# Six transformer layers: the order of pieces in the loops of TensorE, VectorE, ScalarE and GpSimd laid out anew

## What is computed

```
qkv = shift(x) @ Wqkv;  q, k = l2norm(q) * qs, l2norm(k) * ks;  q, k = rotary(q), rotary(k)
p   = softmax(8 * q @ [k_prev_window, k_window] + mask);  x = (p @ [v_prev, v]) @ Wo + x
xn  = layernorm(shift(x)) * g + b;  a, gate = split(xn @ W1 + b1);  x = a * gelu(gate) @ W2 + b2 + x
```

## Time and profile before

| | |
|---|---|
| three runs | 3569.05, 3572.99, 3574.07 us; median 3572.99 |
| the profiled execution | 3574.2 us, span 3572.4 us |
| busy share of the span | PE 94%, PEld 75%, DVE 78%, ACT 71%, POOL 79% |
| mean granted TensorE clock | 0.977 |

### The profile page before, as it was taken

The page is one execution under the profiler, slowest core; times in us unless marked ns, Lnnn a source line. Parts: engine busy times, 40 slices in busy tenths (PEclk is TensorE's granted clock), DMA queues, the critical chain, the costliest instruction groups (busy, mean ns, idle before and its releaser), DMA issues.

```text
span 3572.4 us, 148602 instructions
## 1 busy us (share of the span) xinstructions
PE 3355.3 (94%) x64228; PEld 2680.4 (75%) x64228; DVE 2803.0 (78%) x4876; ACT 2546.0 (71%) x4688; POOL 2810.5 (79%) x3469
## 2 busy tenths in 40 slices
PE   4798897999999999999999999999999999999997
PEld 2555554778788888787888888887888887888875
DVE  3386667888888888888888888888888888888873
ACT  3333224778788888888887887887888888887863
POOL 1355646988898888898888888888888888888871
PEclk9898999999999999999999999999999999999998
DMA  3332221211121111122111221112111112111110
GB/s 103 103 104 77 86 57 41 57 41 43 40 56 44 48 40 46 40 53 52 44 40 47 51 53 38 43 44 51 46 47 42 41 45 53 40 44 48 38 43 25
DMA packets 126732, 183.45 MB, mean 51 GB/s; under 512 B 29824, under 2 KB 61440, under 8 KB 126080
## 3 DMA queue, kind: packets, MB, share of 16 engines
q1 hardware_dynamic: 119232, 146.15, 16.3%
q0 software_dynamic: 6848, 27.80, 2.6%
HBM read 59.01 MB, written 14.16 MB: 20 GB/s over the span
## 4 chain that ended last, share of the span: by engine, by line
PE 82%; POOL 6%; issue 4%; DVE 3%; ACT 2%; DMA 1%; another core or an unknown queue 0%; SPq 0%; POOLq 0%; ACTq 0%; DVEq 0%
PE bank L565 21%; PE bank L628 10%; PE bank L639 9%; PE bank L601 7%; PE bank L575 5%; PE bank L585 5%; PE bank L612 4%; PE bank L702 3%; PE bank L680 3%; PE bank L691 3%; PE bank L478 1%; PE bank L538 1%; PE bank L648 1%; PE bank L517 1%; PE bank L543 1%
## 5 line engine op out<-in xcount | busy, mean ns | idle before, releaser
L565 PE MATMUL bank<-wqkv,xs 128*128 128x512 f32 x3456 | 1045.2, 420 | 8.3 <-DVE m L1096 5.1
L1868 POOL TENSOR_TENSOR m<-m 128x512 f32<-128x512 f32 x576 | 753.0, 1316 | 28.1 <-DVE m L1096 27.5
L565 PEld LDWEIGHTS bank<-wqkv,xs 128*128 128x128 f32 x3456 | 590.2, 191 | 99.7 <-DVE m L1096 7.2
L1107 DVE TENSOR_REDUCE ss<-sq 128x8 f32<-128x512 f32 x768 | 505.8, 670 | 98.1 <-ACT sq L1465 97.7
L1096 DVE TENSOR_TENSOR m<-bank,tab 128x512 f32<-128x512 f32 x768 | 521.5, 679 | 2.5 <-POOL m L1868 2.5
L1465 ACT ACTIVATE sq<-bank 128x512 f32<-128x512 f32 x768 | 454.6, 599 | 64.8 <-PE bank L565 45.3
L1876 POOL TENSOR_TENSOR S<-S,nw 128x1024 f32<-128x1024 f32 x192 | 367.5, 1914 | 112.0 <-DVE S L1127 107.7
L628 PEld LDWEIGHTS bank<-P,big 64*64 64x64 f32 x24576 | 378.8, 135 | 94.6 <-issue 93.5
L1884 POOL TENSOR_TENSOR S<-S,rs 128x512 f32<-128x512 f32 x384 | 396.3, 1048 | 32.1 <-DVE rs L1141 31.6
L1094 DVE TENSOR_TENSOR m<-bank,tab 128x512 f32<-128x512 f32 x576 | 391.7, 680 | 36.2 <-PE bank L585 19.5
L628 PE MATMUL bank<-P,big 64*64 64x32 f32 x24576 | 401.9, 220 | 7.0 <-issue 6.5
(11 more groups left out here) (229 smaller groups left out, 6566.5 us busy)
## 6 DMA issues: line engine op xcount, KB each, us to landing
big<-vst SPq DMA_DIRECT2D x1536, 64.0 KB, 2.0
stage<-in_wqkv SPq DMA_DIRECT2D x36, 256.0 KB, 3.0
tab<-in_tab SPq DMA_DIRECT2D x48, 128.0 KB, 2.2
xsort<-big SPq DMA_DIRECT2D x4, 960.0 KB, 8.4
wo<-in_wo SPq DMA_DIRECT2D x6, 512.0 KB, 3.6
big<-xsort SPq DMA_DIRECT2D x12, 256.0 KB, 6.6
ysort<-big SPq DMA_DIRECT2D x12, 256.0 KB
big<-in_x SPq DMA_DIRECT2D x8, 256.0 KB, 4.2
```

Of the source, the lines that this page charges most:

```text
L565: m = eng.matmul(pb[:, :], xt[a], wqkv[:, z, 512 * part:512 * part + 512], start=(n == 0), stop=(n == 2))
L1107: eng.tensor_reduce(ss[:, g // 2 % 2, a:a + 8], sq[:, part % 2, :].rearrange("p (h d) -> p h d", d=DH), axis=X_AX, op=ALU.add).then_inc(s[ ...
L1868: eng.tensor_tensor(turned(g, part), turned(g, part), m2[:, part % 2, :], ALU.add).then_inc(s["g_add"], 1)
```

## The change

It reorders calls in the four branches of the four loops, and moves a few calls across the loops' ends so that each piece is still done once. No function, instruction, bank or buffer changes. A call that reads `f(n - 1, ...)` in one branch and `f(n, ...)` in the branch before it is the same piece at nearly the same place; what really moves is less than the diff looks. Cut to its core:

```
@@ TensorE, q4 == 0 @@
                     turn_q(n, 1)
                     proj(n + 1, 0)
                     probs(n - 3, 0)
-                    proj(n + 1, 1)
                     probs(n - 3, 1)
@@ q4 == 1 @@
+                    proj(n, 1)
+                    out_proj(n - 5)
...
                     proj(n, 5)
+                    sim(n - 2)
                     gate(u - 4, 2)
-                    sim(n - 2)
@@ q4 == 2 @@
                     up(u - 4, 2)
+                    spread(u - 3)
                     proj(n, 2)
-                    spread(u - 3)
                     turn_k(n - 2, 0)
+                    turn_k(n - 2, 1)
                     proj(n, 3)
-                    turn_k(n - 2, 1)
                     proj(n, 5)
@@ VectorE, q4 == 1 (before: low(u + 1) stood in q4 == 3) @@
                     residual(n - 5)
+                    low(u + 1)
+                    summed(n - 3)
+                    inverted(n - 3)
+                    rotate(n, 1)
@@ q4 == 3 (before: xn_low(u - 4) stood in q4 == 0, between largest and lessened) @@
                     summed(n - 3)
+                    weights(n, 1)
                     inverted(n - 3)
-                    weights(n, 1)
+                    xn_low(u - 3)
+                    rotate(n, 2)
+                    rotate(n, 3)
+                    weights(n, 2)
+                    reduced(n, 2)
@@ ScalarE, q4 == 0 @@
                     weights(n - 1, 4)
+                    masked(n - 2)
                     square(n, 1)
-                    masked(n - 2)
-                    exps(n - 3)
-                    weights(n - 1, 5)
                     v_out(n, 0)
@@ q4 == 1 @@
+                    exps(n - 4)
+                    square(n - 1, 2)
                     turned_k(n - 3, 0)
-                    square(n - 1, 2)
+                    out_turned(n - 5, 0)
                     turned_k(n - 3, 1)
                     square(n - 1, 3)
+                    out_turned(n - 5, 1)
                     v_out(n - 1, 1)
...
                     probs(n - 4, 1)
-                    square(n, 0)
+                    masked(n - 2)
                     square(n, 1)
...
                     turned_k(n - 2, 1)
-                    masked(n - 2)
@@ q4 == 2: shifted from before exps to behind v_out @@
                     v_out(n, 0)
                     shifted(u - 2)
-                    exps(n - 3)
-                    v_out(n, 0)
@@ GpSimd, q4 == 1 and 2 (before: tables in q4 == 1, scale(n - 1, 0) between the adds) @@
                     add(n, 0)
+                    add(n, 1)
+                    tables(u + 1)
+                    divide(n - 3, 0)
+                    divide(n - 3, 1)
```

More of the change, by code:

```diff
@@ L795, in _ @@
                     turn_q(n, 1)
-                    probs(n - 3, 0)
-                    proj(n + 1, 1)
                 elif q4 == 2:
+                    probs(n - 4, 0)
+                    proj(n, 1)
                     probs(n - 4, 1)
@@ L833, in _ @@
                     sim(n - 2)
+                    end_variance(u - 5)
+                    turn_q(n, 0)
             for par in range(2):
@@ L1232, in _ @@
             reduced(0, 1)
+            reduced(0, 2)
+            rotate(0, 2)
+            rotate(0, 3)
             for n in range(1, NG + 2):
@@ L1628, in _ @@
                 if q4 == 0:
+                    out_turned(n - 5, 0)
+                    weights(n - 1, 2)
+                    v_out(n - 1, 1)
+                    weights(n - 1, 3)
+                    high(u + 1)
+                    turned_q(n - 1, 0)
+                    out_turned(n - 5, 1)
                     turned_q(n - 1, 1)
                     probs(n - 4, 0)
-                    weights(n - 1, 3)
                     square(n, 0)
@@ L1680, in _ @@
                     turned_k(n - 2, 1)
+                    square(n, 3)
                     out_turned(n - 4, 0)
-                    v_out(n, 1)
-                    square(n, 3)
-                    out_turned(n - 4, 1)
-                    turned_q(n, 0)
-                    square(n + 1, 0)
-                    turned_q(n, 1)
-                    probs(n - 3, 0)
+                else:
+                    v_out(n - 1, 1)
+                    out_turned(n - 5, 1)
+                    turned_q(n - 1, 0)
+                    weights(n, 0)
+                    turned_q(n - 1, 1)
+                    probs(n - 4, 0)
+                    square(n, 0)
+                    probs(n - 4, 1)
                     scaled(u - 3)
-                else:
-                    probs(n - 4, 1)
-                    xn_high(u - 3)
-                    weights(n, 0)
                     square(n, 1)
                     weights(n, 1)
-                    masked(n - 2)
+                    xn_high(u - 3)
                     exps(n - 3)
                     centred(u - 2)
-                    out_turned(n - 4, 0)
+                    masked(n - 2)
                     end_centred(u - 5)
@@ L1705, in _ @@
                     square(n, 3)
-                    weights(n, 2)
-                    v_out(n, 1)
-                    high(u + 2)
-                    turned_q(n, 0)
-                    out_turned(n - 4, 1)
-            out_turned(NG - 3, 0)
-            out_turned(NG - 3, 1)
             scaled(NU - 3)
@@ L1905, in _ @@
             add(0, 1)
+            add(0, 2)
+            add(0, 3)
             for n in range(1, NG + 2):
```

192 lines of the change are left out of this document (93 added, 99 removed).

## The result

| | before | changed kernel |
|---|---|---|
| median of 4 runs each on one chip | 3573.53 us | 3612.68 us |
| ratio, 95% interval | | 1.0107, 1.0092 to 1.0122 |
| profiled execution, span | 3572.4 us | 3610.7 us |

A forecast was written before the change was run, and what follows sets the result against it. A TensorE queue full to within some tenths of a microsecond a unit was taken as the bound. Terms of -0.08 us a unit gave -4 us, first units -2: -6 from the median, 3567 us, range 3548 to 3588.

The forecast's parts named there:

- The step that failed: TensorE ahead of `sim`: 18.5 us idle for "issue" in 2000 us, no other engine late, untouched by reordering.
- the sign of this case: Sign of a wrong prediction: a unit over 60 us without the new waits for `rotate` or `v_out`.
- `spread` against `v_out`, +0.15: Third tile, TensorE: `spread` must wait until `v_out` empties bank 2, starting at 2045.13 instead of 2044.98: +0.15 us a unit.
- The second `turn_k` earlier, -0.14: Third tile, TensorE: one projection earlier, so ScalarE has its bank emptied before `sim`: -0.14 us a unit.
- `masked`, -0.10: Second tile: `masked` earlier on ScalarE, `sim` ahead of the last gate; 0.79 us from gate to `sim` becomes 0.69: -0.10.
- `xn_low`, -0.11: VectorE pass taken out of GpSimd's chain: `scale` 0.47 us earlier, the wait of `turn_k` goes, -0.11 us a unit.
- `low` at 0: VectorE pass moved to the second tile, between `residual` and the second `rotate`: 0 us a unit, +0.3 at the far end.
- the slow rival that I priced: Second tile: `low` waits behind GpSimd, `rotate` ends too late for a projection; 0.3 us a unit, 3581 us; chance 0.25.
- ScalarE's +0.12: Four places where ScalarE's slack shrinks, among them `v_out` and `turned_q` delayed by `out_turned`: +0.03 us each, +0.12 a unit.
- ScalarE's +0.02: ScalarE's new order in a unit: +0.12 us for shrunken slack less 0.10 for the earlier `masked`.

The follow-up runs named there:

- gate back: The changed kernel with TensorE doing the last gate ahead of `sim` again in the second tile, as before: ratio 1.0016 to the kernel before.
- `masked` alone: The kernel before with only `masked` moved behind `probs` on ScalarE in the second tile: ratio 1.0072 to the kernel before.

## Why the prediction was wrong

**The step that failed** is a sentence in its first part: the "issue" time ahead of `sim` is "time in which no other engine is shown as late; reordering takes none of that away". I took it for a constant, so that the sum had no term for it. It is the time for which TensorE's next block of instructions is late, and its size depends on when the last separate wait ahead of a dense piece goes through. Two things came with a move that I priced at -0.10 us: with `sim` ahead of the last gate, the wait for `turned_k` moved from the gate to `sim`, and with it came a separate wait instruction; the last one ahead of the scores now goes through 1.03 us ahead of them instead of 2.92. That is +0.79 us a unit, 36 us for 46 units; taking it back returned 33. The prediction did name the sign of this case, "a longer unit than 60 us with none of these [waits], which would mean that the 'issue' time moved", but gave it no chance and no price. The earlier trace rows held a bound: a stop of up to 1.7 us in each of the 33 units of the 2000 us, for a piece that was moved.

**The terms of the sum, in a unit.**

- `spread` against `v_out`, +0.15: the wait is right, its size is not. In the kernel before, the projection at this place starts 0.70 us behind `up` (2044.28 to 2044.98), and `spread` now starts after 0.95 (means of the units): +0.25. `v_out` ends at 2131.04 and `spread` starts at 2131.18, so the step from the one to the other took 0.14 us, where I had put 0.05. Before:

```profile
2044.28 0.86 PE L691 MATMUL bank<-xnr,w1r 128*85 128x512 f32 x3
```

After:

```profile
2130.24 0.86 PE L691 MATMUL bank<-xnr,w1r 128*85 128x512 f32 x3
2131.18 0.62 PE L667 MATMUL bank<-kc,nw 128*128 128x128 f32 x4
```

```profile
2130.44 0.60 ACT L1478 ACTIVATE vst<-bank 128x512 f32<-128x512 f32 x1 [1.60 <-PE bank L565]
```

- The second `turn_k` earlier, -0.14: right (last projection to `sim` 0.93 before, 0.79 after). The tile still lost 0.18, where these two terms gave +0.01: beside `spread`'s 0.10 more, `proj` part 2 now stands behind the four transposes of `spread` and takes 0.79 us instead of 0.70. That price was in the earlier trace rows, and I did not apply it.
- `masked`, -0.10: wrong. With the mask done 8 us ahead (gate back, and `masked` alone) the gate still gives way to `sim` after 0.78 us; 0.69 was what a projection takes, not a gate. The row showed a wait of 0.4 us on the weight load, and it was all covered. With `masked` moved alone, the 33 cases of it in the earlier trace rows are gone and the idle time of `sim`'s weight loads for "issue" went from 16 cases to 48.
- `xn_low`, -0.11: right for the chain, wrong for TensorE. `turn_k` starts 0.80 us behind its projection instead of 0.86 in the mean of the units, but the median was 0.80 and is 0.81. So 0.80 us is what this projection takes with no wait at all, and the 0.69 that I held it against is not its free time. The mean gains from the few units in which `turn_k` really waited for `scale`: 5 cases of together 1.7 us in 2000 before, none after. VectorE's and GpSimd's rows before and after, 1050 to 3050 us (count, busy us, mean ns):

```profile
L1158 DVE TENSOR_TENSOR xs<-xf,xs 128x512 fp32r<-128x512 f32 x33 | 36.6, 1110 | 0.0
...
L1182 DVE TENSOR_TENSOR xnr<-xn,xnr 128x512 fp32r<-128x512 f32 x33 | 22.4, 680 | 0.0
...
L1835 POOL TENSOR_TENSOR nw<-nw 128x72 f32<-128x72 f32 x66 | 35.2, 533 | 5.2
```

```profile
L1158 DVE TENSOR_TENSOR xs<-xf,xs 128x512 fp32r<-128x512 f32 x33 | 27.3, 828 | 0.2 <-issue 0.2
...
L1182 DVE TENSOR_TENSOR xnr<-xn,xnr 128x512 fp32r<-128x512 f32 x32 | 20.1, 627 | 0.0
...
L1836 POOL TENSOR_TENSOR nw<-nw 128x72 f32<-128x72 f32 x66 | 22.4, 339 | 5.2
```

The chain's step no longer takes 0.8 us (at most 0.4), and `low` is shorter too. The change did what it says, and TensorE had almost nothing to gain from it.

- `low` at 0: right; no projection waited for its `rotate`, and the slow rival that I priced did not happen. ScalarE's +0.12: about 0; the slack of `turn_q` behind `v_out` fell from 0.61 to 0.14 us and held.

With the last gate alone put back, all these terms together gave 1.0016, +6 us where I had -6; with the third tile put back as well, 1.0003. The loss was outside the sum. That the rest of the sum came out within 12 us (0.3%) was in part luck: the terms gave VectorE's and GpSimd's new orders -0.11 us a unit and ScalarE's +0.02, and alone they cost 0.86% and 0.76%, some 0.67 and 0.59 us a unit; only together do they come to nothing.

## What to carry to other kernels

When a list of waits says "issue" in front of many small instructions, ask where the next block of instructions comes from, and how far ahead of the piece the last separate wait goes through. Give a dense piece one carried wait, call the late semaphore first and drop what an in-order engine implies, and keep a long piece with few instructions (here the last gate) between the last separate wait and the dense piece. And price a reordering as a whole: here two sets of moves that cost 0.8 to 0.9% each cost nothing together.

## What the hardware showed that I had not expected

- TensorE's instructions come in packets of 256; from a packet's start to the first instruction behind the border it takes 2.16 us or more, and a stop leaves TensorE idle for up to 2.6 us. With scores matmuls starting every 10 ns, one such time is as long as 200 of them.
- One more wait instruction in one piece of a unit of 60 us: 0.55% of the kernel. The same two waits in the other order: 1.5% more, about half of it through the clock, which was at its lower level for 61.4 us instead of 6.8 in groups 20 to 176.
- A late packet starts 1.1 to 1.2 us (medians of five kernels) behind the last separate wait of TensorE, and not at one fixed distance in instructions from the border. What makes it start there, and why it starts well ahead of the wait in other units, is not settled.
- A pass of two SBUF inputs moved with the schedule again: with the gate and the third tile put back, `xn_low` takes 1595 ns in the mean instead of 627, and the ratio is still 1.0003.

```profile
L1182 DVE TENSOR_TENSOR xnr<-xn,xnr 128x512 fp32r<-128x512 f32 x33 | 52.6, 1595 | 0.0
```
